# Attention in steps of one query tile and four heads, on fp32 row strips, with the other products between the steps

## The reference

```python
# layer 0 (x is the residual)
hidden = gelu(x @ down_W.T + down_b)
hidden = hidden @ Wsel.T + bsel + domain_emb[idx]      # by sequence
x = layernorm(hidden @ up_W.T + up_b + x) * ln_gamma + ln_beta
# layer 1
x = _ln(x) * (1 + scale) + shift                       # from the timestep
q, k, v = x @ Wq + bq, x @ Wk + bk, x @ Wv + bv        # 16 heads of 32
scores = einsum('bhqd,bhkd->bhqk', q / sqrt(32), k) + attention_bias
scores = where(src_mask, -inf, scores)
ctx = softmax(scores) @ v
x = x + (ctx @ Wo + bo)
x = x + _gelu2((_ln(x) * g2 + beta2) @ W1 + b1) @ W2 + b2
# layer 2: x = layernorm(gelu(x @ Wi[e] + bi[e]) @ Wo[e] + bo[e] + x) * gamma[e] + beta[e]
# layer 3: f + dt * stencil(A_grid, B_grid, f), cut off below at 0
```

## Time and profile before

| | us |
|---|---|
| median of 3 runs (2885.51 to 2888.85) | 2886.93 |
| the profiled execution's own time | 2886.56 |
| its span, first to last instruction | 2884.7 |
| PE busy (share of the span) | 2538.6 (88%) |
| DVE busy | 2074.9 (72%) |
| ACT busy | 1192.5 (41%) |
| POOL busy | 945.4 (33%) |

### The profile page before, as it was taken

The page is one execution under the profiler, slowest core; times in us unless marked ns, Lnnn a source line. Parts: engine busy times, 40 slices in busy tenths (PEclk is TensorE's granted clock), DMA queues, the critical chain, the costliest instruction groups (busy, mean ns, idle before and its releaser), DMA issues.

```text
span 2884.7 us, 44452 instructions
## 1 busy us (share of the span) xinstructions
PE 2538.6 (88%) x12843; PEld 1240.9 (43%) x12923; DVE 2074.9 (72%) x3941; ACT 1192.5 (41%) x2229; POOL 945.4 (33%) x896
## 2 busy tenths in 40 slices
PE   3789898988888898984999999999999999999992
PEld 1344444444444444442444444444444444444440
DVE  4575847576666667576886878868788687886877
ACT  2474747475665657473332322323223223232221
POOL 3322231222131313123433434334343343433426
PEclk8899999999999999996999999999999999999995
DMA  4454545453535454544322223222232222322222
GB/s 133 147 162 137 169 129 168 132 165 128 167 131 165 139 163 147 148 154 155 129 94 85 96 92 111 87 80 95 92 110 88 88 85 92 110 88 89 86 72 80
DMA packets 182947, 345.52 MB, mean 120 GB/s; under 512 B 20354, under 2 KB 50690, under 8 KB 182674
## 3 DMA queue, kind: packets, MB, share of 16 engines
q1 hardware_dynamic: 172882, 324.31, 35.3%
q10 hardware_dynamic: 9792, 17.83, 1.7%
HBM read 298.85 MB, written 17.86 MB: 110 GB/s over the span
## 4 chain that ended last, share of the span: by engine, by line
PE 37%; issue 7%; DVE 5%; POOL 4%; ACT 1%; DMA 0%; SPq 0%; DVEq 0%; POOLq 0%; ACTq 0%
PE ffn_bank L1305 12%; PE ffn_bank L1307 11%; PE ffn_bank L1306 11%; POOL prod L1226 2%; PE ffn_bank L1298 2%; POOL f L1216 1%; POOL x L1244 1%; PE ffn_bank L1364 1%; DVE g2T_hi L1598 0%; PE ffn_bank L1314 0%; DVE tmp L1507 0%; ACT g L1426 0%; DVE g2T_lo L1599 0%; DVE tmp L1547 0%; DVE tmp L1499 0%
## 5 line engine op out<-in xcount | busy, mean ns | idle before, releaser
L930 DVE CUSTOM_DVE_ANT_0 negs<-bank,bias 128x512 f32<-128x512 f32 x512 | 341.6, 686 | 153.5 <-PE bank L604 130.0
L737 ACT ACTIVATE prob<-negs,nmax 128x512 f32<-128x512 f32 x512 | 366.1, 716 | 133.9 <-DVE nmax L930 128.3
L614 PE MATMUL bank<-ident,prob 128*128 128x128 f32 x2048 | 335.7, 292 | 64.6 <-ACT prob L737 35.3
L614 PEld LDWEIGHTS bank<-ident,prob 128*128 128x128 f32 x2048 | 265.2, 150 | 208.1 <-ACT prob L737 57.9
L1598 DVE CAST g2T_hi<-g 128x512 f16<-128x512 f32 x256 | 190.7, 745 | 154.7 <-ACT g L1426 150.0
L1599 DVE TENSOR_TENSOR g2T_lo<-g,g2T_hi 128x512 f16<-128x512 f32 x256 | 272.2, 1063 | 8.8
L1426 ACT ACTIVATE g<-ffn_bank,bi 128x512 f32<-128x512 f32 x128 | 88.0, 687 | 361.4 <-PE ffn_bank L1307 331.1
L1305 PE MATMUL ffn_bank<-w_hi,g2T_hi 128*128 128x512 f16 x512 | 197.1, 385 | 24.7 <-DVE g2T_lo L1599 24.5
L604 PE MATMUL bank<-k_st,q_st 96*128 96x512 f16 x512 | 206.3, 403 | 8.6 <-issue 4.8
L1226 POOL TENSOR_TENSOR prod<-grid,f 128x512 f32<-128x512 f32 x108 | 167.2, 1574 | 124.6 <-DMA grid<-in_grids 118.5
L603 PE MATMUL bank<-mask_add,ident_bf 128*128 128x512 bf16 x432 | 171.7, 397 | 40.4 <-DVE nmax L930 40.4
(11 more groups left out here) (257 smaller groups left out, 5054.0 us busy)
## 6 DMA issues: line engine op xcount, KB each, us to landing
bias<-in_bias SPq DMA_DIRECT2D x256, 512.0 KB, 3.6
raw<-in_W_l SPq DMA_DIRECT2D x128, 512.0 KB, 3.3
grid<-in_grids SPq DMA_DIRECT2D x172, 256.0 KB, 3.5
q_st<-pT SPq DMA_DIRECT2D x96, 128.0 KB, 5.5
k_st<-pT SPq DMA_DIRECT2D x96, 128.0 KB, 2.9
xin<-in_x SPq DMA_DIRECT2D x9, 1024.0 KB, 5.3
x2n<-x_rows SPq DMA_DIRECT2D x9, 1024.0 KB, 7.0
out<-outt ACTq DMA_DIRECT2D x36, 256.0 KB, 2.1
```

The costliest lines, as they stand in the source:

```text
L614: mm = pe.transpose(bank[:, t * P:(t + 1) * P], prob[:, h % 2, t, j * P:(j + 1) * P], ident[:, :])
L737: act.activation(prob[:, h % 2, j, :], negs[:, j % NT, :], ACT.Exp, scale=-1.0, bias=nmax[:, h % 2, j:j + 1], accum_out=rsum[:, j, h:h + 1 ...
L930: dve.tensor_tensor_reduce(negs[:, j % NT, :], bank[:, :], bias[:, half % NB, j % 2, :], -1.0, 3.0e38, ALU.add, ALU.min, nmax[:, h % 2, j: ...
```

## The change

- The unit of work becomes a step u of 16: query tile j = u % 4 of the four heads of group g = u // 4. Its four scores lie in banks 0 to 3. PE first writes four masks, then four fp32 products of 32 rows each: head i of the group has rows 32i to 32i+31 of `q32` and `k32`, the layout in which the projections come out. The fp16 split of q and k, `q_st`, `k_st` and their 24 transfers go. ACT brings q to fp32, DVE k.
- Only q, k and v of group or tile 0 stand ahead of the steps. The other projections, `xT`, `down`, `expert`, `up` and the transposes of 1/sum are placed between a step's scores and the rest by `BESIDE`. They and the transposes of probabilities share banks 4 to 6. The value sums go by pairs of steps (256 columns), kb by kb between later steps, all in bank 7.
- A step is, on PE: scores of u, `BESIDE[u]`, value sums, the four transposes of step u-1. DVE copies two of them after its scores and pieces, ACT the other two at the places in `TURNED`. LayerNorm statistics are at u = 6 and 10 behind each score on DVE, scalings at u = 8, 9 and 12, 13.
- The exponential is in place, in `tiles` (a ring of three steps). `x1T` has memory of its own. The output goes to `x2t`, part of `tiles`, so that POOL waits for the evacuation of the output products and not for the store; DVE waits for the store at u = 1.
- x is loaded in four pieces, each behind POOL's addition for it. A bias chunk is two heads of one query tile instead of one head of two query tiles, of the same size.
- Output products of groups 0 and 1 go into step 17, those of 2 and 3 behind the transposes of the next x1.

```diff
+NQ = G * T
+SLOTS_ALL = NQ + 4
+NR = 3
+def pv_parts(u):
+    return [(v, kb) for v in range(NQ // 2) for kb in range(T) if 2 * v + 3 + kb // 2 == u]
+BESIDE = {0: [("v", 1), ("xT", 0), ("xT", 1)], 1: [("v", 2), ("xT", 2), ("xT", 3)],
+          2: [("v", 3), ("down",), ("q", 1)], 3: [("expert",), ("k", 1)], 4: [("up", 0), ("up", 1)],
+          5: [("R", 0), ("up", 2), ("up", 3)], 6: [("q", 2)], 7: [("k", 2)], 9: [("R", 1)], 10: [("q", 3)],
+          11: [("k", 3)], 13: [("R", 2)], 17: [("R", 3)]}
+TURNED = {0: (4, 4), 1: (4, 4), 2: (4, 4), 3: (4, 4), 4: (2, 4), 5: (2, 4), 6: (4, 4), 7: (4, 4), 10: (4, 4), 11: (4, 4)}
+ACT_L0 = {33 + t: ("scale0", t) for t in range(T)} | {49 + t: ("scale1", t) for t in range(T)}
+DVE_L0 = {24 + t: ("stats0", t) for t in range(T)} | {40 + t: ("stats1", t) for t in range(T)}
+PROLOGUE_DVE = [("g",), ("e",)] + [(name, t) for name in ("y", "stats0", "stats1") for t in range(T)]
...
+    for u in range(SLOTS_ALL):
+        if u < NQ:
+            order += [(("S", u, i), i) for i in range(4)]
+        for v, kb in pv_parts(u):
+            if v % 2 == 0 and kb == 0:
+                order.append((("ctx", v // 2), 7))
+        keys = BESIDE.get(u, []) + ([("T", u - 1, i) for i in range(4)] if 0 < u <= NQ else [])
+        for key in keys:
+            order.append((key, 4 + ring % 3))
             ring += 1
-        if 0 <= n - LAG_T < HT:
-            m = n - LAG_T
...
-    order = [(("q", c), c) for c in range(C)]
-    order += [(("k", c), 4 + c) for c in range(C)]
-    order += [(("v", t), t) for t in range(2)]
-    order += [(("xT", c), 4 + c) for c in range(C)]
-    order += [(("v", t), t) for t in range(2, T)] + [(("down",), 4)]
+    order = [(("q", 0), 4), (("k", 0), 5), (("v", 0), 6)]
     order += attention_slots()
-    order += [(("x1T", c), 3 + c) for c in range(C)]
-    order += [(("wo", t), (0, 1, 2, 7)[t]) for t in range(T)]
+    order += [(("x1T", c), 4 + c) for c in range(C)]
+    order += [(("wo", t), t) for t in range(T)]
...
-        q_st = sb("q_st", [P, H, S], F16)
-        k_st = sb("k_st", [P, H, S], F16)
+        q32 = sb("q32", [P, C, S], F32)
+        k32 = sb("k32", [P, C, S], F32)
...
-        negs = sb("negs", [P, NT, S], F32)
-        nmax = sb("nmax", [P, 2, T], F32)
+        tiles = sb("tiles", [P, 4 * NR, S], F32)
+        nmax = sb("nmax", [P, 2, 4], F32)
...
+        x1T = [sb(f"x1T_{h}", [P, C, S], F16) for h in ("hi", "lo")]
+        x2t = tiles[:, 4:8, :]
...
-                    src = a["bias"][it, h, j * 2 * P:(j + 1) * 2 * P, :].rearrange("(t p) s -> p t s", p=P)
+                    u, h = n // 2, 4 * (n // 8) + 2 * (n % 2)
+                    src = a["bias"][it, h:h + 2, (u % T) * P:(u % T + 1) * P, :].rearrange("h p s -> p h s")
...
-                sp.wait_ge(x1b_ready, it * T + T)
                 sp.wait_ge(x1_hi, it * C + C)
-                load_x(nxt)
+                sp.sem_inc(sp_carrier, 1)
+                for t in range(T):
+                    sp.wait_ge(x1b_ready, it * T + t + 1)
+                    sp.sem_inc(sp_carrier, 1)
+                    load_x(nxt, t)
                 sp.wait_ge(x1_ready, it * T + T)
                 load_expert(bass.ds(nxt, 1))
                 load_ada(nxt)
                 sp.wait_ge(mask_ready, it * 1 + 1)
                 load_mask(nxt)
-                for which, (parts, stack) in enumerate(((qT, q_st), (kT, k_st))):
-                    sp.wait_ge(qk_split, it * 2 * C + (which + 1) * C)
-                    for i in range(4):
-                        for slot in SLOTS:
-                            sp.dma_start(
-                                stack[32 * slot[0]:32 * slot[0] + 32, :, :].rearrange("p (c i) s -> p i c s", i=4)[:, i],
-                                parts[slot[1 + which]][32 * i:32 * i + 32, :, :]).then_inc(qk_stacked, 16)
...
-                pool.wait_ge(x2_out, 1 + it * 64)
                 for t in range(T):
+                    pool.wait_ge(x2_ready, it * T + t + 1)
                     pool.wait_ge(x1_ready, it * T + t + 1)
...
+                def scores(u):
+                    g, j = u // T, u % T
+                    if u == 0:
+                        pe.wait_ge(mask_ready, it * 1 + 1)
+                    if j == 0:
+                        pe.wait_ge(q32_ready, it * C + g + 1)
+                        pe.wait_ge(k32_ready, it * C + g + 1)
+                    for i in range(4):
+                        bank = claim(pe, it, ("S", u, i))
                         pe.matmul(bank[:, :], ident_bf[:, :], mask_add[:, j, :], start=True, stop=False)
-                        pe.matmul(bank[:, :], q_st[0:96, h, j * P:(j + 1) * P], k_st[0:96, h, :],
-                                  start=False, stop=True).then_inc(full_of(("S", h, j)), 1)
...
+                    for i in range(4):
+                        rows = slice(HD * i, HD * i + HD)
+                        pe.matmul(psum[i][:, :], q32[rows, g, j * P:(j + 1) * P], k32[rows, g, :],
+                                  start=False, stop=True).then_inc(full[i], 1)
+                def values(v, kb):
+                    g = v // 2
+                    if kb == 0:
+                        if v % 2 == 0:
+                            claim(pe, it, ("ctx", g))
+                        pe.wait_ge(v32_ready, 1 + it * T + T)
+                        for half in range(2):
+                            pe.wait_ge(pT_ready[half], 1 + it * (HT // 2) + 4 * v + 4)
+                    cols = slice((v % 2) * 2 * P, (v % 2) * 2 * P + 2 * P)
+                    for i in range(4):
+                        h = 4 * g + i
+                        mm = pe.matmul(psum[7][HD * i:HD * i + HD, cols], v32[:, kb, h * HD:(h + 1) * HD],
+                                       pT[:, v % 2, i, kb, :], start=kb == 0, stop=kb == T - 1)
+                    if kb == T - 1:
+                        mm.then_inc(pv_done, 1)
+                def turn(u, i):
+                    pe.wait_ge(prob_ready, 1 + it * HT + 4 * u + i + 1)
+                    bank = claim(pe, it, ("T", u, i))
+                    for t in range(T):
+                        mm = pe.transpose(bank[:, t * P:(t + 1) * P], tiles[:, 4 * (u % NR) + i, t * P:(t + 1) * P],
+                                          ident[:, :])
+                    mm.then_inc(full_of(("T", u, i)), 1)
...
+                pe.wait_ge(x1T_split, it * C + C)
+                for key in (("q", 0), ("k", 0), ("v", 0)):
+                    project(key)
+                for u in range(SLOTS_ALL):
+                    if u < NQ:
+                        scores(u)
+                    for key in BESIDE.get(u, []):
+                        if key[0] in ("q", "k", "v"):
+                            project(key)
+                        elif key[0] == "R":
+                            spread(key[1])
+                        else:
+                            l0_products(it, key)
+                    if u == NQ + 1:
+                        out_products(0)
+                        out_products(1)
+                    for v, kb in pv_parts(u):
+                        values(v, kb)
+                    if 0 < u <= NQ:
+                        for i in range(4):
+                            turn(u - 1, i)
+                for c in range(C):
+                    l0_products(it, ("x1T", c))
+                out_products(2)
+                out_products(3)
...
+                def evacuate(u, i):
+                    bank = arrived(act, it, ("T", u, i))
+                    act.wait_ge(pv_done, 1 + it * (NQ // 2) + max(0, u // 2 - 1))
+                    act.activation(pT[:, (u // 2) % 2, i, :, (u % 2) * P:(u % 2 + 1) * P],
+                                   bank[:, :].rearrange("p (t q) -> p t q", t=T), ACT.Copy).then_inc(pT_ready[0], 1)
+                for u in range(SLOTS_ALL):
+                    places = TURNED.get(u, (1, 3))
+                    for i in range(5):
+                        n = 4 * u + i
+                        if i == min(3, places[0]):
+                            for key in BESIDE.get(u, []):
+                                take(key)
+                        for k in range(2):
+                            if i == places[k] and 0 < u <= NQ:
+                                evacuate(u - 1, 2 * k)
+                        if i == 4:
+                            break
+                        if u < NQ:
+                            tile = tiles[:, 4 * (u % NR) + i, :]
+                            h, j = 4 * (u // T) + i, u % T
+                            act.wait_ge(scored, 1 + it * HT + n + 1)
+                            act.activation(tile, tile, ACT.Exp, scale=-1.0, bias=nmax[:, u % 2, i:i + 1],
+                                           accum_out=rsum[:, j, h:h + 1]).then_inc(prob_ready, 1)
+                        if n in ACT_L0:
+                            l0_part(it, ACT_L0[n])
+                        for g in range(G - 1):
+                            if u == 4 * g + 7 and i == 0:
```

(41 more changed lines are left out.)

297 lines of the change are left out of this document (88 added, 209 removed).

## The result

The kernel after takes 2899.0 us (median of 7 runs, 2893.95 to 2900.39), the kernel before 2887.2 in the same comparison (7 runs). The ratio is 1.0036, 95% interval 1.0026 to 1.0045: slower by some 10 us, where 14 us less were forecast. The profiled execution took 2895.3 us, its span is 2893.5.

The account below looks back on a forecast made before the run. PE's own work was to bound the attention loop: 136.5 us an iteration, 150.5 with waits, 152.2 with clock falls, against 154.0 now. Eight iterations gave -14.4 us from 2886.6, so 2872 us; range 2800 to 2940.

Parts of the forecast that it names:

- All else, 1652.7 us of the span, I take as unchanged: Everything outside the attention pass's loop over eight sequences would keep its time, 1652.7 us of 2884.7.
- the clock's term: Attention loop: PE's clock at half speed for 6.8 us in every second iteration, adding 1.7 us to 150.5.
- Row strips: PE's scores: four fp32 products on 32 rows each take 1.2 us a group; bounds 1.0 and 3.4 us.
- Rival 2: PE's row strips overlap badly: 1.7 us a group, 2936 us in all; not at all, 3150 us; chance 0.15.
- Value sums: On PE, 32 groups of 256 columns instead of 16 of 512: 0.57 us each, 18.4 us against 16.0 before.
- The plain step: An attention step without extra work, carried by PE: 5.3 us; forecast wrong if u=8, 14, 15 are not near it.
- Start: Iteration's opening through the first k copy: 10.0 us, expert load 4.8 us behind POOL's adds, PE waiting 2.2 us.
- The waits at u=2, 6 and 10: PE waits among the transposes for banks: 2.0 us at u=2, 1.8 each at u=6 and 10 with LayerNorm statistics.
- the last 1/sum turn: Iteration's end: 1.5 us for copy and reciprocal before PE's last transposes of 1/sum, within an end of 19.5 us.
- Rival 1: Two clock falls per attention iteration, in steps PE carries: 157.3 us an iteration, 2913 us in all; chance 0.18.
- PE's share: PE's busy share in the attention loop was to be over 0.92.
- the granted clock: PE's granted clock in the attention loop was to be 0.98; 0.95 or less would point to Rival 1.

Follow-up runs that it names:

- the increments: Idle semaphore increments on DVE ahead of the FFN loop: 8 on the kernel after, 2884.0 us; 120 on the kernel before, 2902.4 us.
- experiment 5: Kernel after with 8 idle DVE increments; DVE takes first k before the expert's weights, now built at u=2 behind its scores: 2853.0 us.
- experiment 4: Kernel after with 8 idle DVE increments, plus either expert's weights moved behind k to u=1 (2877.1 us) or statistics two a step, scalings later (2876.7).

## Why the prediction was wrong

**The step that failed first** is "All else, 1652.7 us of the span, I take as unchanged". The other code was unchanged, its time was not: 11.7 us in the FFN loop, because DVE's shorter attention loop moved a boundary of its code in front of a cast that races POOL's product. The Trainium skill, "Runtime: NRT & Kernel Launch", Instruction fetch mechanics, has it that each engine's code streams in blocks of 16 KiB, 256 instructions, and that crossing into the next costs little, mostly hidden. Queue 8's packets have that size (1.52 MB in 93, 16.3 KB each); queue 14's, which go with DVE's instructions, are 8.2 KB (1.02 MB in 125), and the increments fit 128 instructions, so for DVE the measurement decides. The crossing is short here too, 0.29 us where no wait hides it, but at one place it turned the order of two operations. The prediction had no such rival: none of the rows it read shows a crossing, though the kernel before has one in every FFN iteration, ahead of number 373.

**The second step that failed** is the clock's term, "I count one in every second iteration, 1.7 us". It was 2.8 us, as follows.

**The iteration.** Mean lengths of seven iterations after, from masks to masks, beside the forecast's terms; the last row is the mean of those iterations in which no fall touched the step (the first iteration left out; sums are of unrounded lengths):

```
                 start  u0   u1   u2    u3   u4   u5   u6    u7   u8   u9   u10   u11  u12  u13  u14  u15+end+return   sum
forecast         10.0   5.7  8.7  13.9  8.5  7.0  7.0  9.6   7.8  5.3  6.6  9.6   7.8  5.3  6.6  5.3  25.8            150.5
measured         10.8   6.1  8.7  13.9  8.7  7.2  7.1  10.0  8.4  4.7  7.3  10.1  8.6  4.7  7.3  4.7  25.1            153.6
without a fall   10.9   5.3  8.7  13.9  8.7  7.2  7.1  9.9   7.6  4.7  7.3  9.9   7.6  4.7  7.3  4.7  25.1            150.8
```

- Row strips: 1.2 forecast, 1.07 measured. Rival 2 is out. Value sums 1.01 for 1.15, masks with change 0.96 as forecast, transposes with change 1.92 for 1.85. The plain step is 4.7 to 5.0 for 5.3: right in kind, 0.3 to 0.6 too long. Single terms miss by up to 0.9 either way and cancel; that the sum without falls is met to 0.3 is in part luck.
- Start: k's copy from 9.8 to 10.6 us (557.67 less 547.84, and 0.74 more) for 10.0; POOL's adds end at 3.8 for 3.1 and the expert load comes 4.5 later for 4.8. The copy was held up by the very transfer that was named. PE's wait is 3.13 for 2.2, since a step of masks begins 1.2 us behind the start of the k copy.
- The waits at u=2, 6 and 10 are there, 1.9, 2.0 (1.14 and 0.82) and 2.0 us, for 2.0, 1.8 and 1.8, and 1.5 before the last 1/sum turn as forecast; those of u=9 and 13, 0.5 us before the 1/sum turn and 0.9 behind it, make these steps 0.7 too long.
- Clock: 15 falls in the loop, 54.6 us, or 6.8 us per iteration at half speed; I had put 6.8 us in every second one. Their price can be read off, since a step without a fall repeats to 0.1 us from iteration to iteration, but for the start and the end: step 7 takes 7.6 us without a fall and 9.2 with one of 3.4 us that lies in it, so a fall costs half its length. Iterations with 3.4 us of falls take 151.9 and 152.8 us, the one with 13.7 takes 157.0. Without falls the sum is 150.8 for the forecast's 150.5; with them it is 153.6. This is the size that was off, 2.8 us for 1.7. What I missed is that four of eight iterations have a fall behind the start's gap and all eight one in steps 6 and 7 or 10 and 11. Rival 1 had the mechanism, with twice the length of a fall.
- PE's share is 137.6 of 154 us, 0.89, not 0.92; the granted clock 0.98 as forecast.
- The last iteration was not a term of the sum: before, it lies within the same 166 us up to POOL's first FFN operation as after (167), so eight savings were counted where seven can show.

So the attention pass gave 2.8 us of 14.4 in the profiled run: 7 x 0.5, and 1 us back in the last iteration. Of the 1.4 us per iteration that are missing, the clock term's miss is 1.1 and the steps' own 0.3. Most of the falls don't hang on the start's gap: in experiment 5 its end took the loop's falls from 15 (54.6 us, the same in the kernel with the increments alone) to 12 (41.0), but all of that difference is in the last iteration. In the seven others they only moved (to steps 3, 7 and 11), and the 2 us a period that were gained are the gap itself; of the 8 us in the last iteration some 5 are the clock, half of 10.2 us less at half speed. Two slips in the recorded sums move nothing: 32 x 0.57 is 18.2 and not 18.4, and row strips without overlap would be 282 us and not 270.

**What stays open:** why a late cast brings a clock fall at step 3 of every FFN iteration rather than of every second one, and whether the 4 and 5 us of the two edits of experiment 4 are more than what separates runs.
